# Layer sums from two matmuls, first weights in quarters, and a reordered end in a two-layer cross-attention kernel

## What is computed

```python
# layer 0
Q = query @ Wq + bq;  K = key @ Wk + bk;  V = key @ Wv + bv
weights = softmax(Q @ K.T * 512 ** -0.5, axis=-1)
x = query + (weights @ V) @ Wo + bo
# layer 1, emb = x in 8 x 2048 rows (the attention is per sequence of 256)
q = emb @ Wq + bq;  k = latent @ Wk + bk;  v = latent @ Wv + bv
w = softmax(q @ k.T * 512 ** -0.5, axis=1)          # over the query rows
x = w @ v + emb
out = (x - mean(x)) * rsqrt(var(x) + EPS) * gamma + beta
```

## Time and profile before

| | us |
|---|---|
| median of 3 runs (lowest to highest) | 1176.57 (1173.44 to 1177.16) |
| time of the profiled execution | 1174.09 |
| its span | 1172.3 |
| PE busy | 1147.3 (98%) |
| DVE, ACT, POOL busy | 899.4, 855.1, 961.2 |
| chain that ended last: share of PE | 94% |

### The profile page before, as it was taken

How to read it: one execution, slowest core, us unless ns; L and a number is a source line. 1 busy time by engine, 2 the same in 40 slices (tenths; PEclk the granted TensorE clock), 3 DMA queues, 4 the chain that set the end, 5 groups by cost and what they waited for, 6 DMA issues and landing times.

```text
span 1172.3 us, 25323 instructions
## 1 busy us (share of the span) xinstructions
PE 1147.3 (98%) x8001; PEld 1070.1 (91%) x8001; DVE 899.4 (77%) x2081; ACT 855.1 (73%) x1733; POOL 961.2 (82%) x767
## 2 busy tenths in 40 slices
PE   9989999999999999999999999999999999999985
PEld 7879999999999999999999999999999999999974
DVE  2667787787777778778778778777777877877887
ACT  2557777777777777777777777777777778777763
POOL 2458898898898888889889889889888888988864
PEclk9999999999999999999999999999999999999998
DMA  8455666666666666666667666666666666666631
GB/s 337 165 189 200 216 223 221 213 233 204 223 230 206 225 230 211 217 221 218 221 212 222 219 214 235 201 224 238 196 227 226 215 218 218 222 221 213 196 105 75
DMA packets 131551, 249.04 MB, mean 212 GB/s; under 512 B 15680, under 2 KB 88896, under 8 KB 123072
## 3 DMA queue, kind: packets, MB, share of 16 engines
q1 hardware_dynamic: 130512, 247.59, 62.7%
q10 hardware_dynamic: 1008, 1.06, 0.3%
HBM read 165.16 MB, written 83.43 MB: 212 GB/s over the span
## 4 chain that ended last, share of the span: by engine, by line
PE 94%; DVE 2%; ACT 1%; issue 1%; DMA 1%; POOL 1%; SPq 0%; POOLq 0%; DVEq 0%; ACTq 0%
PE bank L366 90%; PE bank L444 2%; PE bank L506 1%; PE bank L513 1%; PE bank L533 1%; DMA PT_raw<-E_dram 0%; SPq L255 0%; DVE R L981 0%; ACT bank L760 0%; DMA gT<-g_dram 0%; POOLq L69 0%; DVE y_blk L989 0%; POOL Y L1397 0%; ACT Y L788 0%; DVE w_lo L1032 0%
## 5 line engine op out<-in xcount | busy, mean ns | idle before, releaser
L1336 POOL TENSOR_TENSOR xT_lo<-IN,xT_hi 128x1024 fp32r<-128x1024 f32 x64 | 154.5, 2414 | 21.0 <-ACT xT_hi L652 21.0
L1336 POOL TENSOR_TENSOR yT_lo<-yT_raw,yT_hi 128x1024 fp32r<-128x1024 f32 x63 | 149.9, 2380 | 18.6 <-ACT yT_hi L652 17.3
L1397 POOL TENSOR_TENSOR Y<-Y,gamma_b 128x512 f32<-128x512 f32 x126 | 160.5, 1297 | 3.0 <-ACT Y L788 3.0
L1400 POOL TENSOR_TENSOR Y<-Y,beta_b 128x512 f32<-128x512 f32 x126 | 161.2, 1302 | 0.0
L788 ACT ACTIVATE Y<-R,nmr,rstd 128x512 f32<-128x512 f32 x126 | 96.0, 810 | 74.6 <-POOL nmr L1384 74.6
L366 PE MATMUL bank<-yT_hi,A_hi 128*128 128x256 f32 x512 | 144.6, 282 | 1.1 <-issue 1.1
L366 PE MATMUL bank<-xT_hi,A_hi 128*128 128x256 f32 x512 | 144.6, 282 | 1.1 <-DVE A_lo L1124 1.1
L1382 POOL TENSOR_TENSOR rstd<-ve,half 128x2 f32<-128x2 f32 x63 | 44.5, 707 | 123.3 <-DVE nmu L1080 123.3
L366 PE MATMUL bank<-xT_hi,A_lo 128*128 128x256 f32 x512 | 144.6, 282 | 0.0
L366 PE MATMUL bank<-yT_lo,A_hi 128*128 128x256 f32 x512 | 144.4, 282 | 0.0
L366 PE MATMUL bank<-xT_lo,A_hi 128*128 128x256 f32 x512 | 144.2, 282 | 0.0
(11 more groups left out here) (130 smaller groups left out, 4242.1 us busy)
## 6 DMA issues: line engine op xcount, KB each, us to landing
IN<-in_packed SPq DMA_DIRECT2D x64, 1024.0 KB, 5.0
R<-in_x SPq DMA_DIRECT2D x64, 512.0 KB, 4.3
y_dram<-y_blk SPq DMA_DIRECT2D x252, 128.0 KB, 2.5
yT_raw<-y_dram SPq DMA_DIRECT2D x63, 512.0 KB, 3.5
out<-Y SPq DMA_DIRECT2D x63, 512.0 KB, 2.6
E_dram<-E_blk SPq DMA_DIRECT2D x256, 64.0 KB, 1.7
PT_raw<-E_dram SPq DMA_DIRECT2D x64, 256.0 KB, 2.7
gT<-g_dram SPq DMA_DIRECT2D x64, 128.0 KB, 3.8
```

What stands on the lines that cost most here:

```text
L1336: return nc.gpsimd.tensor_tensor(dst, src, fp(hi), ALU.subtract)
L1397: nc.gpsimd.tensor_tensor(y[:, q, :], y[:, q, :], gamma_b[:, :], ALU.mult).then_inc(Y_mul, 1)
L1400: last = nc.gpsimd.tensor_tensor(y[:, q, :], y[:, q, :], beta_b[:, :], ALU.add)
```

## The change

**Start.** Layer 0's Wq and Wk come in one array W0 in four transfers by quarter h; A0_product is called once for each quarter and waits for its quarter alone. Sequence 0's input comes in two transfers: xT behind the first quarter, the rest behind the fourth. The low part of xT(0) is made half by POOL and half by DVE. The warm-up is 11 matmuls of 512 columns in place of 32 of 128. The later start-up transfers (WvT0, IN(1), WkT1, WqT1, x), the Bv product and S0(0), some steps on ACT, DVE and POOL, and the place of the identity tile change their order. On SP, load_IN(4) now stands ahead of read_E0(1).

**Row sums.** ACT writes w's second half once more in fp32 (w_1), DVE adds the first half to it (w_sum), ACT takes the hi part of that (w_sums_h), POOL the low part (w_sums_l, in place of w_low_sum), and `s_` is two matmuls. In `body`, s_ stands ahead of wc_. ACT's cT_h moves ahead of w_1_ and w_h, u_h behind xT_h; DVE's E0_blocks and x1(r+2, 0) move ahead of variances, w_sum_ is put behind variances, w_l behind x1(r+2, 1), s_columns ahead of v_l; POOL's cT_l moves ahead of scales.

**End.** The lists of the last four sequences are reordered on every engine; the last layer norm is worked in halves, and its centred rows are written to PSUM (`centre`).

```diff
@@ PE
-                pe.wait_ge(w_los_set, n.count())
-                for t, part in enumerate((w[0][:, 0, :], w[0][:, 1, :], w_los[:, :])):
-                    last = nc.tensor.matmul(s_bank[:, 0:S], ones[:, :], part, start=(t == 0), stop=(t == 2))
+                pe.wait_ge(w_sums_lo, n.count())
+                for t, part in enumerate(w_sums):
+                    last = nc.tensor.matmul(s_bank[:, 0:S], ones[:, :], part[:, :], start=(t == 0), stop=(t == 1))
...
-                for _ in range(32):
-                    nc.tensor.matmul(bank[0][:, 0:P], ones[:, :], ones[:, :], start=True, stop=True)
+                for _ in range(11):
+                    nc.tensor.matmul(bank[0][:, :], ones[:, :], flat(vT[0]), start=True, stop=True)
...
+            def A0_product(h):
+                pe.wait_ge(w0_in[h], 16)
                 for n in range(2):
-                    A_part(bank[6 + n], WqT0_s, WkT0_s, n, (0, 1))
...
+                    last = A_part(bank[6 + n], WqT0_s, WkT0_s, n, (h,))
...
+                s_(r)
                 wc_(r)
-                s_(r)
...
             S1_(T(3))
             pred_(T(2), 0)
             pred_(T(2), 1)
+            wc_(T(3))
             s_last()
-            wc_(T(3))
@@ ACT
+            def w_1_(n):
...
+                act.wait_ge(rz1_set, n.count())
+                first(act, w_sum_set, n.count(back=1))
+                copy(w_1[:, :], S1_bank[:, S:2 * S], scale=rz1[:, 1:2]).then_inc(w_1_set, 1)
+
+            def w_sums_h(n):
...
+                act.wait_ge(w_sum_set, n.count())
+                first(act, s_full, n.count(back=1))
+                copy(w_sums[0][:, :], w_sum[:, :]).then_inc(w_sums_hi, 1)
@@ DVE
+            def w_sum_(n):
...
+                dve.wait_ge(w_1_set, n.count())
+                dve.wait_ge(w_hi, n.count())
+                first(dve, w_sums_lo, n.count(back=1))
+                nc.vector.scalar_tensor_tensor(w_sum[:, :], S1_bank[:, 0:S], rz1[:, 0:1], w_1[:, :], ALU.mult, ALU.add
+                                               ).then_inc(w_sum_set, 1)
...
+            def centre(q):
+                dve.wait_ge(nmu_last, q + 1)
+                nc.vector.scalar_tensor_tensor(bank[2 + q][:, :], R[T(3).k % 4][:, q, :], nmu[:, q:q + 1], gamma_b[:, :],
+                                               ALU.add, ALU.mult).then_inc(centred, 1)
@@ POOL
+            def w_sums_l(n):
...
+                pool.wait_ge(w_sums_hi, n.count())
+                minus(w_sums[1][:, :], w_sum[:, :], w_sums[0][:, :]).then_inc(w_sums_lo, 1)
...
                 yT_l(r.plus(1))
+                cT_l(r.plus(4))
                 scales(r.plus(-1))
-                cT_l(r.plus(4))
-                w_low_sum(r)
+                w_sums_l(r)
...
+            plus_beta(T(2), 0)
+            plus_beta(T(2), 1)
+            scales_last(0)
+            scales_last(1)
```

More of the change, by code:

```diff
@@ L122, in build @@
         gT = sb("gT", [P, 1, S])
-        w_los = sb("w_los", [P, S], f32r)
+        w_1 = sb("w_1", [P, S])
+        w_sum = sb("w_sum", [P, S])
+        w_sums = split("w_sums", [P, S])
         scol = sb("scol", [P, ST, 32])
@@ L730, in S1_seed_ @@
                 first(act, w_lo, n.count(back=1))
+                if n.ends():
+                    act.wait_ge(w_sum_set, n.count(back=1))
                 copy(S1_bank[:, :].rearrange("p (a b) -> p a b", a=ST), gT[:, :, :].to_broadcast([P, ST, S])
@@ L852, in _ @@
             C_h(Seq(2))
+            A1_h(1)
             u_h(Seq(2))
             xT_h(Seq(3))
+            out_seed_(Seq(1))
+            PT_h(Seq(1))
             cT_h(Seq(3))
+            u_h(Seq(3))
+            C_h(Seq(3))
+            Pc_h(Seq(1))
             exps0(Seq(2))
[L857 to L861 removed]
             yT_h(Seq(0))
@@ L881, in body @@
                 exps0(r.plus(3))
+                cT_h(r.plus(4))
+                w_1_(r)
                 w_h(r)
-                cT_h(r.plus(4))
+                w_sums_h(r)
                 normalise(r.plus(-1))
@@ L933, in _ @@
             w_h(T(3))
+            normalise(T(1))
             wc_h(T(3))
@@ L1030, in w_l @@
                 dve.wait_ge(w_hi, n.count())
+                if n.ends() and n.plus(1).there():
+                    dve.wait_ge(w_1_set, n.count())
                 for m in range(ST):
@@ new lines, in spread, with yT_last_l, add_s @@
+            def spread(n):
+                stats_ready(n)
+                variances(n)
+            def yT_last_l():
+                for q in range(ST):
+                    dve.wait_ge(yT_last_hi, q + 1)
+                    last = minus(yT[1][:, q * DT:(q + 1) * DT, :].rearrange("p a b -> p (a b)"), bank[2 + q][:, :],
+                                 yT[0][:, q * DT:(q + 1) * DT, :].rearrange("p a b -> p (a b)"))
+                last.then_inc(yT_lo, 1)
+            def add_s(q):
+                y = R[T(3).k % 4][:, q, :]
+                dve.wait_ge(s_set, T(3).count())
+                nc.vector.scalar_tensor_tensor(y, bv1_b[:, :], scol[:, q, 0:1], y, ALU.mult, ALU.add
+                                               ).then_inc(s_added, 1)
@@ L1294, in _ @@
             Pc_l(T(3))
+            w_sum_(T(1))
             spread(T(0))
-            s_columns(T(1))
+            wc_l(T(1))
             x1(T(3), 0)
-            wc_l(T(1))
             x1(T(3), 1)
@@ L1303, in _ @@
             v_l(T(2))
+            s_columns(T(1))
             yT_last_l()
@@ L1308, in _ @@
             w_l(T(2))
+            w_sum_(T(2))
+            v_l(T(3))
             x2(T(1), 1)
             moments(T(1))
-            spread(T(1))
-            v_l(T(3))
             s_columns(T(2))
@@ L1315, in _ @@
             max1(T(3))
+            spread(T(1))
             rz1_(T(3))
@@ L1320, in _ @@
             moments(T(2))
+            spread(T(2))
+            wc_l(T(3))
             s_columns(T(3))
-            wc_l(T(3))
-            spread(T(2))
             add_s(0)
@@ L1326, in _ @@
             x2_last(0)
+            x2_last(1)
             moments_last(0)
-            x2_last(1)
             moments_last(1)
-            spread(T(3))
-            finish_last()
+            spread_last(0)
+            spread_last(1)
+            centre(0)
+            centre(1)
+            finish_last(0)
+            finish_last(1)
         @block.gpsimd
@@ L1367, in yT_l @@
                 minus(blocks(yT[1]), raw(yT_raw), blocks(yT[0])).then_inc(yT_lo, 1)
-            def w_low_sum(n):
+            def w_sums_l(n):
                 if not n.there():
                     return
-                pool.wait_ge(w_lo, n.count())
-                first(pool, s_full, n.count(back=1))
-                nc.gpsimd.tensor_tensor(w_los[:, :], fp(w[1][:, 0, :]), fp(w[1][:, 1, :]), ALU.add
-                                        ).then_inc(w_los_set, 1)
+                pool.wait_ge(w_sums_hi, n.count())
+                minus(w_sums[1][:, :], w_sum[:, :], w_sums[0][:, :]).then_inc(w_sums_lo, 1)
             def scales(n):
```

246 lines of the change are left out of this document (149 added, 97 removed).

## The result

The changed kernel takes 1179.75 us (median of 7 runs, 1179.38 to 1181.17) against 1174.74 us for the kernel before in the same comparison. The ratio is 1.0044, with a 95% interval of 1.0033 to 1.0055, so it is slower by 5.0 us. Forecast were +3.8 us and "just slower". That the forecast time of 1180.4 us lies within 0.7 us of the measured one is partly luck: the forecast was added to 1176.57 us, the kernel before came out at 1174.74 here, and the difference was 1.2 us larger than forecast. The spans of the profiled executions are 1177.6 us after and 1172.3 before, 5.3 us apart.

A forecast was written before the change was run, and what follows sets the result against it. PE, busy throughout the steady part, was taken as the bound. Loop +9.6, start -4.5 and end -1.3 gave +3.8 us, so the median 1176.57 becomes 1180.4 us; own range 1176 to 1185, 8 in 10 from 1165 to 1188.

The forecast's parts named there:

- Part 1, the wait at the row sums: Steady loop: s_ saves a 0.12 us matmul but waits 0.28 us for w_sums_lo; +9.6 us over 60 iterations.
- the step on it: At wc in the loop: late w_lo costs nothing behind the waiting s, about 0.2 us without that wait.
- that rival: Loop: the sums come in time, waits at s_ and for w_lo vanish, -7.2 us there, 1163.6 us total; chance 0.15.
- The hold on ve: DVE in the loop: ve held until POOL's cT_l ends; wait 0.25 us, against 0.16 without the hold.
- Part 2, the start: Up to S1(0): earlier first u, at 14 to 15 us, and shorter waits; -4.5 us, bounds -1.2 and -6.2.
- The product at full pace: A0 product at the start: all 32 matmuls at the fast pace take 6.4 us.
- the waits between 50 and 72 us: PE's four idle waits before the steady part, 6.77 us: one or two go, about 1.5 us gained (0 to 2.5).
- The step that the shift is kept: Start: Bv and u(1) follow the first u without a gap, so its shift is kept.
- Part 3, the end: Last four sequences: PE's waits shrink but POOL ends last; -1.3 us, bounds 0 and -3.
- some 0.9: End: only some 0.9 us of PE's gain gets through, as POOL's queue is filled by T(1)'s later steps.
- centre, with two SBUF inputs, is held by GpSimd: End, on DVE: centre reads R and gamma_b from SBUF, so by the skill's port-sharing rule GpSimd holds it.
- The halves give back 0.4: End: working the last layer norm in halves gives back 0.4 us of the last steps.

The follow-up runs named there:

- f1: The changed kernel with VectorE's w_sum ahead of the variances; 1216.88 us (single run), period 18.16 us.
- g1: The changed kernel with wc ahead of s on TensorE and v_l ahead of s_columns on VectorE in the loop; 1180.73 us (single run).
- g2: g1 with VectorE's w_lo also ahead of the second x1; 1163.68 us (5 runs), ratio 0.9912 to the kernel before.
- f4: The changed kernel with GpSimd's cT_lo behind rstd, nmr and w_sums_lo instead of ahead of them; 1183.5 us (single run), period 17.58 us.
- f12: f1 with GpSimd's w_sums_lo also taken ahead of rstd and nmr; 1216.58 us (single run), period 18.12 us.
- k1: The changed kernel's start and end with the loop of the kernel before; 1172.07 us (10 runs), ratio 0.9976 to the kernel before.
- h2: The changed kernel with the first quarter of A0's product also waiting for the last quarter of the weights; 1186.79 us (single run).
- t1: The changed kernel with T(3)'s second residual kept in PSUM, where moments_last and centre read it; 1178.44 us (single run).

## Why the prediction was right, and where it was not

**Part 1, the wait at the row sums: right.** The chain held row by row. Shifted by the 0.96 us between the two iterations (E_blk at 613.31 and 614.27), the forecast had rstd at 616.29, w_sums_lo at 617.22 and w_lo at 617.18; measured were 616.30, 617.23 and 617.19. The cost was forecast as 0.28 - 0.12 = 0.16 us per iteration, and the period grew by 0.16. The exact match has some luck in it: the wait itself is 0.22 and not 0.28 us (0.25 by the rows), and the other 0.06 come from starts further apart in v, pred and out, which the forecast didn't have. f1 shows that GpSimd's queue sets w_sums_lo. g1 shows that w_lo was just hidden behind the waiting s, as the step on it said. g2 shows the price of the one-matmul gain, two chains earlier, as forecast for that rival. Its time is met by luck (1163.6; g2 took 1163.7): 13.0 us less than 1176.57 were forecast, and g2 takes 10.4 less than 1174.1, since start and end bring less than forecast and the loop 6.4 us (by the traces) and not 7.2.

**The hold on ve: right, and its worth was read as more than it is.** ve was to be held until cT_lo ends; it ended at 616.16 where cT_lo ended at 616.12, and f4 takes the hold away and 0.12 us with it. The text gave the loop without the hold a wait of 0.16 in place of 0.25 us. That difference holds at this seam only. f4 and f12 show that GpSimd has less than 1 us to spare once around, up to PT_lo. The rivals of the prediction didn't have this one: a gain at the seam paid back at Pc.

**Part 2, the start: right in kind, 0.9 us too much.** Two terms of it were mis-sized. The product at full pace was taken as 6.4 us, from 27 rows in 5.31 us times 32. A window also counts rows that only reach into it: 24 of the 27 are starts of the product. It has 32 rows in every trace, and they start 0.216 us apart at the full clock, which makes 6.9 us; k1's, all at the full clock, took 6.91. In the changed kernel it took 7.27, as the clock came up 0.74 us behind its start. The first u came at 15.31 and not at 14 to 15. And the waits between 50 and 72 us gave back 0.6 and not 1.5 us: PT_lo's 0.86 went and S1(0)'s 1.87 became 0.73, but that of v(0), for the round trip of y, grew from 1.12 to 2.51. The forecast said that this wait stays, and priced none of its growth. The step that the shift is kept was right, and h2 shows it at 6.85 us for 6.85.

**Part 3, the end: -0.2 for -1.3 us.** PE went better than forecast: 1.35 us less from u(T3) to the last matmul. Behind the last matmul it went the other way, 11.31 us for the 10.20 of before. What ends last is GpSimd's queue, as the prediction said, and its rows, first before and then after, give the terms:

```profile
1161.80 2.49 POOL L1397 TENSOR_TENSOR Y<-Y,gamma_b 128x512 f32<-128x512 f32 x2 [0.93 <-ACT Y L788]
```
```profile
1167.26 2.48 POOL L1501 TENSOR_TENSOR Y<-Y,gamma_b 128x512 f32<-128x512 f32 x2 [0.93 <-ACT Y L824]
```

The failed step is "some 0.9" of PE's gain getting through. Behind u(T3), gamma of T(2) started 57.03 us before and 56.93 after, so 0.1 got through: rstd of T(2) stands behind T(1)'s beta in GpSimd's queue until 1164.91, where before it started as soon as its input was there. A second term was put at nothing: the prediction said that centre, with two SBUF inputs, is held by GpSimd, and didn't ask what centre does to GpSimd. rstd starts 3.34 us behind the start of beta where it started 2.90 behind it, 0.44 more; t1 takes 0.9 of beta's 3.38 us away. "The halves give back 0.4" was right in kind and gave 0.6: VectorE's last step starts 0.64 us behind the start of rstd and not 1.23. Together -0.1 + 0.44 - 0.6, the measured -0.2.

**The sum.** +3.8 and +5.3 us in the trace, +5.0 (3.9 to 6.5) by the medians. The verdict rested on part 1 alone, and that was the part with rows for every step.

## What to carry to other kernels

When an edit saves a matmul on a full TensorE and makes its operand later, list every operand that is due at the seam, not the latest one only: here two were late by a quarter of a microsecond, moving one brought nothing, and moving both turned +5 us into -10. A move in the queue of an engine at 86% is paid for once around the loop, so follow that engine's queue until the next place where TensorE waits for it, and at the end of the program follow SyncE's queue as well. A warm-up is judged by the pace of the work behind it, counted in starts per microsecond, and not by the clock column, which reads 1.00 here also where the trace has no record.
